# Gate and up of a feed-forward layer in two passes: plain products for the first half of the tokens, seven block products for the second, with weights and forms of x kept in DRAM

## The chip, the cores and the metric

The kernel runs on one core of one Trainium2 chip. The metric is the device time of one execution in microseconds, as the median of several runs. TensorE is PE in the profile, its weight loads PEld, VectorE is DVE, ScalarE is ACT, GpSimd is POOL and SyncE, which issues all transfers, is SP (SPq).

## The reference, cut to what matters

```
x = x + xattn(layernorm(x), ctx, ctx)        # 16 batches of 128 channels x 1024
h = layernorm(x)                             # 2048 tokens x 1024 features
Wg, Wu, Wd = NF4[codes] * scales             # 2752 x 1024, 2752 x 1024, 1024 x 2752; a scale for each 64 inputs
gate = einsum('bsh,ih->bsi', h, Wg)
up   = einsum('bsh,ih->bsi', h, Wu)
out  = x + einsum('bsi,hi->bsh', silu(gate) * up, Wd)
```

Everything is float32. The 2752 rows of the gate and up weights are 21 chunks of 128 and a half chunk of 64, which gate and up share.

## The kernel before

Three stages follow one another. The **mixer** is the attention: 16 batches, one per turn, on all engines; each turn ends with eight transposes of the normalized batch (x2), which ACT copies to `xh` in TensorE's rounded format and from which DVE makes the remainder `xl` (L823). The **gate and up stage** multiplies every chunk by the 2048 tokens, in four blocks (tb) of 512 tokens. A float32 product is three matmuls: weight high part by x high part, weight high by x low, weight low by x high (`products`, L1069 to L1071), eight times for the 1024 inputs. So 43 items (gate and up of 21 chunks, and the shared one) take 43 x 4 x 24 = 4128 matmuls. The **down stage** takes 40 groups of seven block products of six matmuls (`product`, L1116 to L1118) and 160 matmuls for the rest (L1125 to L1129). Its seven products stand for eight: sums of blocks of the stationary and moving operands are multiplied, and ACT (`snapshot`, L717) and DVE (L930) combine the results.

Beside the matmuls of the gate and up stage runs the making of weights. An item's codes and scales are loaded (L335, L340); ACT turns codes to levels in eight bends, each reading the last one's result (L578, L581); DVE multiplies by the scale (`weigh`, L767). For gate and up ACT makes the high part (L591) and DVE the low part (L772). For each finished block ACT takes silu of the gate (L648), DVE multiplies by up (L841), and SP stores the result (`inter`, L398). For the down stage one item of its weights is made per chunk. From two of them (a pair) seven *forms* are made, four of which are differences (`t_forms`); for each, ACT makes the high part (`form_hi`, L661), DVE the low part (`form_lo`, L846), and SP stores both together (L412). There is one buffer for a form, so `form_hi` waits until the store before it has landed (`form_stored`). Odd chunks make three forms, even chunks from 2 on make four: 70 in all.

The order on each engine is the order in which the program writes it down; nothing is reordered by a scheduler. Each engine goes through its own list and stops at the first wait that isn't met. SP does the same with transfers, all of which go through one queue.

## Time and profile before

| | |
|---|---|
| median of 3 runs | 1540.36 us (1540.14 to 1540.9) |
| the profiled execution | 1539.45 us, span 1537.7 us |
| PE busy | 1509.7 us, 98% of the span |
| ACT busy | 921.8 us, 60% |
| DVE busy | 724.2 us, 47% |
| DMA queue | 46.9% of 16 engines' span |

A duration of a matmul contains its way through the array, which the next matmul overlaps. What a matmul costs in a row of them is the distance from one start to the next. The same holds on ACT and DVE, where an instruction starts before the one ahead of it has ended if it doesn't need its result. "Landing" is the time from a transfer's issue on SP to its completion.

### The profile page before, as it was taken

The numbers are of one execution on the slowest core, as the hardware profiler recorded it, in microseconds if no ns is written. First come the engines' busy times: TensorE is split into PE (matmuls) and PEld (weight loads), VectorE is DVE, ScalarE is ACT, GpSimd is POOL, SyncE is SP. The second block draws the span as 40 slices with busy tenths as digits, with TensorE's granted clock in tenths as the row PEclk, the third lists the DMA queues.
The fourth block names the chain that finished last, engine by engine and source line by source line (L and its number), as shares of the span: only waits on it lengthen the run. The fifth ranks groups of instructions, "written<-read, shape, count | busy, mean of one in ns | idle before, by whom it ended". The sixth has DMA issues, their size and how long they took to land.

```text
span 1537.7 us, 18265 instructions
## 1 busy us (share of the span) xinstructions
PE 1509.7 (98%) x7056; PEld 1254.1 (82%) x7056; DVE 724.2 (47%) x1106; ACT 921.8 (60%) x1067; POOL 60.9 (4%) x99
## 2 busy tenths in 40 slices
PE   7999999999999999999999999999989999999998
PEld 6888788888888888888888888888768888888787
DVE  6998322322322222322322232222368888888764
...
DMA packets 115462, 232.93 MB, mean 151 GB/s; under 512 B 8240, under 2 KB 55344, under 8 KB 110896
## 3 DMA queue, kind: packets, MB, share of 16 engines
q1 hardware_dynamic: 115376, 231.77, 46.9%
...
q14 instruction: 30, 0.25, 0.1%
...
## 4 chain that ended last, share of the span: by engine, by line
PE 92%; ACT 4%; DMA 2%; issue 1%; DVE 1%; SPq 0%; DVEq 0%; POOL 0%; ACTq 0%
PE bank L1071 20%; PE bank L1069 20%; PE bank L1070 20%; PE bank L1116 8%; PE bank L1117 8%; PE bank L1118 8%; PE bank L1020 3%; PE bank L1047 1%; PE bank L1054 1%; DMA F<-inter_scratch 1%; PE bank L1037 1%; ACT early L602 1%; DMA inter_scratch<-F 1%; ACT F L615 1%; ACT F L636 1%
## 5 line engine op out<-in xcount | busy, mean ns | idle before, releaser
L1069 PE MATMUL bank<-R 128*128 128x512 f32 x1376 | 535.9, 389 | 0.0
L1070 PE MATMUL bank<-R 128*128 128x512 f32 x1376 | 535.7, 389 | 0.0
L1071 PE MATMUL bank<-R 128*128 128x512 f32 x1376 | 535.7, 389 | 0.0
L581 ACT ACTIVATE F<-F 128x1024 f32<-128x1024 f32 x441 | 467.6, 1060 | 13.3
L1070 PEld LDWEIGHTS bank<-R 128*128 128x128 f32 x1376 | 258.3, 188 | 53.7
L1071 PEld LDWEIGHTS bank<-R 128*128 128x128 f32 x1376 | 258.3, 188 | 53.6
L1069 PEld LDWEIGHTS bank<-R 128*128 128x128 f32 x1376 | 258.4, 188 | 53.3
L717 ACT COPY F<-bank 128x512 f32<-128x512 f32 x120 | 70.5, 587 | 271.0 <-PE bank L1118 267.1
L841 DVE TENSOR_TENSOR F<-F,bank 128x512 f32<-128x512 f32 x84 | 57.6, 686 | 331.1 <-issue 200.0
L648 ACT ACTIVATE F<-bank 128x512 f32<-128x512 f32 x84 | 49.8, 593 | 215.3 <-PE bank L1071 215.2
L767 DVE SCALAR_TENSOR_TENSOR F<-F 128x1024 f32<-128x1024 f32 x63 | 77.2, 1226 | 169.5 <-ACT F L581 169.5
L930 DVE TENSOR_TENSOR early<-early,bank 128x512 f32<-128x512 f32 x168 | 114.9, 684 | 36.0 <-PE bank L1129 23.9
L1118 PE MATMUL bank<-R 128*128 128x512 f32 x320 | 124.6, 389 | 0.0
L772 DVE TENSOR_TENSOR R<-F,R 128x1024 fp32r<-128x1024 f32 x41 | 50.2, 1225 | 154.9 <-ACT R L591 154.9
L846 DVE TENSOR_TENSOR F<-F 128x256 f32<-128x256 f32 (+2 forms) x230 | 121.0, 548 | 3.2 <-ACT F L661 1.1
L930 DVE TENSOR_TENSOR early<-early,F 128x512 f32<-128x512 f32 x120 | 82.6, 689 | 58.4 <-ACT F L717 57.9
L1118 PE MATMUL bank<-FR,R 128*128 128x512 f32 x240 | 94.6, 394 | 0.0
L1116 PE MATMUL bank<-R 128*128 128x512 f32 x232 | 90.6, 390 | 0.0
L1117 PE MATMUL bank<-R 128*128 128x512 f32 x232 | 90.5, 390 | 0.0
L1020 PE MATMUL bank<-ident,F 128*128 128x128 f32 x512 | 64.5, 279 | 9.9 <-DMA F<-in_ctx 5.8
L1116 PE MATMUL bank<-FR,R 128*128 128x512 f32 x168 | 66.5, 396 | 6.8 <-ACT F L717 6.8
L1118 PEld LDWEIGHTS bank<-R 128*128 128x128 f32 x320 | 60.2, 188 | 12.5
...
## 6 DMA issues: line engine op xcount, KB each, us to landing
wf_scratch<-F SPq DMA_DIRECT2D x70, 512.0 KB, 3.5
inter_scratch<-F SPq DMA_DIRECT2D x84, 256.0 KB, 2.3
F<-in_gu_codes SPq DMA_DIRECT2D x41, 512.0 KB, 5.0
F<-in_gu_scales SPq DMA_DIRECT2D x82, 256.0 KB, 4.2
F<-inter_scratch SPq DMA_DIRECT2D x40, 512.0 KB, 3.8
R<-wf_scratch SPq DMA_DIRECT2D x20, 1024.0 KB, 5.9
FR<-wf_scratch SPq DMA_DIRECT2D x15, 1024.0 KB, 5.9
F<-in_d_codes SPq DMA_DIRECT2D x22, 512.0 KB, 4.4
```

The lines of the kernel that those rows point to most:

```text
L581: nc.scalar.activation(y, y, ACT.Prelu, bias=bias, scale=scale, alpha=alpha).then_inc(bent, 1)
L717: nc.scalar.copy(snap[i], bankX[g % 2]).then_inc(ready, 1)
L767: nc.vector.scalar_tensor_tensor(dst, level[s], ZERO, scales[s], ALU.add, ALU.mult).then_inc(w_ready, 1)
L846: return nc.vector.tensor_tensor(out, x, y, ALU.subtract)
L930: return nc.vector.tensor_tensor(y, y, term, ALU.add)
L1020: i = pe.transpose(dst[:, t * P:(t + 1) * P], src[:, t * P:(t + 1) * P], ident[:, :])
L1069: pe.matmul(dst, hi, xh[:, tb, t, :], start=(t == 0), stop=False)
L1070: pe.matmul(dst, hi, xl[:, tb, t, :], start=False, stop=False)
L1071: i = pe.matmul(dst, lo, xh[:, tb, t, :], start=False, stop=(t == HT - 1))
L1116: pe.matmul(dst, h, moving[:, 0, k, :], start=start and k == 0, stop=False, skip_group_check=not start)
L1117: pe.matmul(dst, h, moving[:, 1, k, :], start=False, stop=False, skip_group_check=not start)
L1118: last = pe.matmul(dst, l, moving[:, 0, k, :], start=False, stop=k == 1, skip_group_check=not start)
```

## The change

- Gate and up run in two passes. The **first pass** is the plain one for tokens 0 to 1023 (blocks tb 0 and 1 of each chunk), in a position p for each chunk: 43 x 2 x 24 = 2064 matmuls. The order of the last positions is the table `BLOCKS`. `BX` is 8, half the batches.
- The **second pass** takes tokens 1024 to 2047. A position p is one chunk, gate and up together, as a product of 2 x 2 blocks (gate and up by the two halves of the inputs by the two blocks of tokens) in seven products of 12 matmuls (`pair_product`). The shared half chunk (p = 20, `FPOS`) takes four products; the last position is p = 21, `FULL`. That is 21 x 84 + 48 = 1812 matmuls.
- In the first pass only gate and up weights are made, two items per position, and each is also stored to `w_dram`. DVE and not ACT makes their high parts (`split`). Beside it the seven forms of x for the second half of the tokens are made, in 28 steps through the same one buffer `form`, 24 of which are stored to `xf_dram` and loaded again for the second pass.
- In the second pass a position loads its two weight items from `w_dram` (`load_staged`, 1 MB, one buffer `staged`), DVE makes four sums (`weight_sums`), ACT and DVE make high and low parts of the seven blocks (`wform_hi`, `wform_lo`), each into the slot that the same product of the position before has left. ACT copies three results (`snap1`, `snapq`, `snap2`), DVE adds others (`c11_sum`, `c22_sum`, `c21_sum`), ACT takes silu (`silu_c`, `silu_x`) and DVE multiplies (`pair_out`). The item of down weights per position, its eight bends and all 70 forms and their stores are now all here.
- In the mixer DVE makes `xl` for the first 8 batches only. The down stage has other buffers and banks; its loads are issued in another order.

The core of the diff; `snapq` and `snap2` are like `snap1`, `c22_sum` and `c21_sum` like `c11_sum`:

```diff
+    w_dram = nc.dram_tensor("w_scratch", (GU, P, N), F32).ap()
+    xf_dram = nc.dram_tensor("xf_scratch", (NP, P, 2, HT // 2, WIDE), F32).ap()
...
+        staged = f(4, 2)
+        tform = halves(6) + halves(7)
+        form = [v.bitcast(F32R) for v in halves(12)]
+        silu = halves(13)
+        inter = halves(14)
+        wsums = halves(15) + halves(16)
...
+        FPOS = FULL - 1
+        POS = FULL + 1
+        BLOCKS = [(p, tb) for p in range(FPOS) for tb in range(2)] + [(FPOS, 0), (FULL, 0), (FPOS, 1), (FULL, 1)]
+        NB1 = len(BLOCKS)
...
+        A11, A12, A21, A22 = [staged[:, i * WIDE:(i + 1) * WIDE] for i in range(4)]
+        WS1, WS2, WS3, WS4 = wsums
+        WFORMS = [A11, WS3, WS2, A12, WS1, A22, WS4]
+        pairX = [banks[0][:, 0, :], banks[1][:, 1, :]]
+        pairQ = [banks[0][:, 1, :], banks[2][:, 0, :]]
+        pairW = [banks[1][:, 0, :], banks[2][:, 1, :]]
...
+            def load_staged(p):
+                c = chunk_of(p)
+                if p:
+                    sp.wait_ge(wfl_ready, nth(p - 1, NP - 1))
+                if c == FULL:
+                    sp.dma_start(staged[:, 0:N], w_dram[GU - 1]).then_inc(staged_in, 16)
+                else:
+                    sp.dma_start(staged.rearrange("p (i n) -> p i n", i=2), w_dram[2 * c:2 * c + 2].rearrange("i p n -> p i n")).then_inc(staged_in, 16)
...
+            for p in range(POS):
+                if p:
+                    store_pair_out(p - 1, 1)
+                next_item(WN + 2 + p)
+                if p == KW:
+                    store_rest(0)
+                    sp.wait_ge(form_stored, 16 * 2 * NP)
+                    load_w(0, 0)
+                if p + 1 < POS:
+                    load_staged(p + 1)
+                for tb in range(4):
+                    store_form(p, tb)
...
+            def wform_hi(p, i):
+                if p == POS or i not in used(p):
+                    return
+                if p == 0:
+                    act.wait_ge(*((gate_done, 2 * FPOS + 3) if i < 4 else (up_done, ups_until(NB1 - 1))))
+                else:
+                    act.wait_ge(pair_done, nth(p - 1, i))
+                act.wait_ge(ws_ready, p + 1)
+                if p == FPOS:
+                    src = {0: A11, 1: WS3, 3: A12, 6: WS4}[i]
+                else:
+                    src = WFORMS[i]
+                nc.scalar.copy(wslice[i][:, 0], src).then_inc(wfh_ready, 1)
...
+            def snap1(p):
+                act.wait_ge(pair_done, nth(p, 0))
+                nc.scalar.copy(c11, pairX[p % 2]).then_inc(a1_ready, 1)
...
+                if last:
+                    bend_wd(FPOS, 2, 4)
+                else:
+                    bend_wd(p, 0, 1)
+                snap1(p)
+                form_hi(p, 0)
+                if last:
+                    bend_wd(FPOS, 4, 6)
+                else:
+                    bend_wd(p, 1, 2)
+                snapq(p)
+                form_hi(p, 1)
+                if last:
+                    bend_wd(FPOS, 6, 8)
+                else:
+                    bend_wd(p, 2, 3)
+                snap2(p)
+                if last:
+                    hi_a(0)
+                    hi_s(0)
+                bend_wd(p, 3, 4)
+                form_hi(p, 2)
+                wform_hi(p + 1, 0)
+                bend_wd(p, 4, 5)
+                silu_c(p)
+                wform_hi(p + 1, 1)
+                bend_wd(p, 5, 6)
+                wform_hi(p + 1, 2)
+                form_hi(p, 3)
+                bend_wd(p, 6, 7)
+                wform_hi(p + 1, 3)
+                bend_wd(p, 7, 8)
+            silu_x(FULL)
...
+            def split(n):
+                p, g = w_home(n)
+                par = p % 2
+                dve.wait_ge(w_ready, n + 1)
+                if p == 1:
+                    dve.wait_ge(fwl_ready, SLICES)
+                    dve.wait_ge(fw_stored, 16 * SLICES)
+                else:
+                    dve.wait_ge(up_done, 2 * p - 2)
+                nc.vector.tensor_copy(wgu[:, par, 0, g], w[n % 2]).then_inc(wh_ready, 1)
+                dve.wait_ge(wh_ready, n + 1)
+                nc.vector.tensor_tensor(wgu[:, par, 1, g], w[n % 2], wgu[:, par, 0, g].bitcast(F32), ALU.subtract).then_inc(wl_ready, 1)
...
+            def weight_sums(p):
+                dve.wait_ge(staged_in, 16 * (p + 1))
+                if p == FPOS:
+                    nc.vector.scalar_tensor_tensor(WS3, A11, -2.0, A11, ALU.mult, ALU.add)
+                    nc.vector.tensor_tensor(WS4, A11, A12, ALU.add).then_inc(ws_ready, 1)
+                    return
+                u = 2 * fulls(p)
+                nc.vector.tensor_tensor(WS1, A21, A22, ALU.add).then_inc(ws_step, 1)
+                sub(WS3, A11, A21)
+                dve.wait_ge(ws_step, u + 1)
+                sub(WS2, WS1, A11).then_inc(ws_step, 1)
+                dve.wait_ge(ws_step, u + 2)
+                sub(WS4, A12, WS2).then_inc(ws_ready, 1)
...
+            def c11_sum(p):
+                dve.wait_ge(pair_done, nth(p, 3))
+                dve.wait_ge(a1_ready, fulls(p) + 1)
+                nc.vector.tensor_tensor(c11, c11, pairW[p % 2], ALU.add).then_inc(c11_ready, 1)
...
+            for p in range(POS):
+                half, last = p == FPOS, p == FULL
+                if p:
+                    pair_out(p - 1, 1)
+                for i in range(4, NP):
+                    wform_lo(p, i)
+                if p and not last:
+                    weigh_wd(p)
+                    if p % 2:
+                        t_forms(p)
+                form_lo(p, 0)
+                form_lo(p, 1)
+                if last:
+                    s_forms(0)
+                    weigh_wd(p)
+                    lo_a(0)
+                    c11_sum(p)
+                    lo_s(0)
+                    c22_sum(p)
+                    c21_sum(p)
+                    pair_out(p, 0)
+                    break
+                weight_sums(p + 1)
+                if half:
+                    for i in range(3):
+                        wform_lo(p + 1, i)
+                    pair_out(p, 0)
+                    form_lo(p, 2)
+                    wform_lo(p + 1, 3)
+                    form_lo(p, 3)
+                    continue
+                form_lo(p, 2)
+                c11_sum(p)
+                wform_lo(p + 1, 0)
+                c22_sum(p)
+                wform_lo(p + 1, 1)
+                wform_lo(p + 1, 2)
+                form_lo(p, 3)
+                c21_sum(p)
+                pair_out(p, 0)
+                wform_lo(p + 1, 3)
+            pair_out(FULL, 1)
...
+            def pair_product(p, i, dst, start, stop):
+                wait(pe, wfl_ready, nth(p, i))
+                if p == 0:
+                    if i == DIRECT:
+                        pe.wait_ge(xpl_ready, XSTEPS)
+                    else:
+                        pe.wait_ge(xform_in[i], 16)
+                for j in range(HT // 2):
+                    hi, lo = [wslice[i][:, q, j * P:(j + 1) * P] for q in range(2)]
+                    a, b = start and j == 0, stop and j == HT // 2 - 1
+                    pe.matmul(dst, hi, xform[i][:, 0, j, :], start=a, stop=False, skip_group_check=not start)
+                    pe.matmul(dst, hi, xform[i][:, 1, j, :], start=False, stop=False, skip_group_check=not start)
+                    last = pe.matmul(dst, lo, xform[i][:, 0, j, :], start=False, stop=j == HT // 2 - 1, skip_group_check=not start)
+                last.then_inc(pair_done, 1)
...
+                pair_product(p, 0, X, True, True)
+                if p >= 2:
+                    pe.wait_ge(c21_ready, before)
+                pair_product(p, 1, Q, True, True)
+                pe.wait_ge(a1_ready, fulls(p) + 1)
+                pair_product(p, 2, X, False, True)
+                if p < 2:
+                    pe.wait_ge(blocks_done, 2 * FPOS + 3)
+                else:
+                    pe.wait_ge(c11_ready, before)
+                pair_product(p, 3, W, True, True)
+                pe.wait_ge(a2_ready, fulls(p) + 1)
+                pair_product(p, 4, X, False, True)
+                pe.wait_ge(aq_ready, fulls(p) + 1)
+                pair_product(p, 5, Q, False, True)
+                pe.wait_ge(c22_ready, fulls(p) + 1)
+                pair_product(p, 6, X, False, True)
...
-                if e:
+                if e and e.n < BX:
```

What stands in a row on three engines, before and after. On ACT, for one even chunk before: L578 and L581 are bends, L648 silu, L661 the high part of a form, L591 the high part of a gate or up weight.

```order
L578 ACTIVATE F<-F 128x1024 [waits w_ready,codes_in0]
L581 ACTIVATE F<-F 128x1024 [waits bent] x7
L648 ACTIVATE F<-bank 128x512 [waits blocks_done,gate_done]
L661 CAST F<-F 128x512 [waits form_stored,t_ready]
L578 ACTIVATE F<-F 128x1024 [waits w_ready,codes_in1]
L581 ACTIVATE F<-F 128x1024 [waits bent] x7
L648 ACTIVATE F<-bank 128x512 [waits blocks_done,gate_done]
L661 CAST F<-F 128x512 [waits form_stored,t_ready]
L578 ACTIVATE F<-F 128x1024 [waits w_ready,codes_in0]
L581 ACTIVATE F<-F 128x1024 [waits bent] x3
L591 ACTIVATE R<-F 128x1024 [waits up_done,w_ready]
L581 ACTIVATE F<-F 128x1024 [waits bent] x4
```

On ACT, in an even position of the second pass of the changed kernel (L805 and L808 bends, L857 the high part of a form, L872 the high part of a weight block, L876, L881 and L885 `snap1`, `snapq`, `snap2`):

```order
L805 ACTIVATE F<-F 128x1024 [waits w_ready,codes_in0]
L876 COPY F<-bank 128x512 [waits pair_done]
L857 CAST F<-F 128x512 [waits form_stored,t_ready]
L808 ACTIVATE F<-F 128x1024 [waits bent]
L881 COPY F<-bank 128x512 [waits pairs_out,pair_done]
L857 CAST F<-F 128x512 [waits form_stored,t_ready]
L808 ACTIVATE F<-F 128x1024 [waits bent]
L885 COPY F<-bank 128x512 [waits pair_done]
L808 ACTIVATE F<-F 128x1024 [waits bent]
L857 CAST F<-F 128x512 [waits form_stored,t_ready]
L872 CAST R<-F 128x512 [waits ws_ready,pair_done]
L808 ACTIVATE F<-F 128x1024 [waits bent]
```

The four forms of a position now stand between the snapshots that TensorE waits for, the first two of them ahead of `snap2`.

On DVE before, the end of one chunk and the start of the next (L767 weighs, L772 and L846 low parts, L841 silu by up):

```order
L772 TENSOR_TENSOR R<-F,R 128x1024 [waits wh_ready,w_ready]
L841 TENSOR_TENSOR F<-F,bank 128x512 [waits inter_stored1,up_done,silu_ready]
L846 TENSOR_TENSOR F<-F 128x512 [waits fh_ready]
L767 SCALAR_TENSOR_TENSOR F<-F 128x1024 [waits scales_in0,bent]
L772 TENSOR_TENSOR R<-F,R 128x1024 [waits wh_ready,w_ready]
L841 TENSOR_TENSOR F<-F,bank 128x512 [waits inter_stored0,up_done,silu_ready]
L846 TENSOR_TENSOR F<-F 128x512 [waits fh_ready]
L841 TENSOR_TENSOR F<-F,bank 128x512 [waits inter_stored1,up_done,silu_ready]
L846 TENSOR_TENSOR F<-F 128x512 [waits fh_ready]
```

On DVE in an even position of the second pass (L1050 weighs, L1144 subtractions for low parts of forms and weight blocks and for sums, L1205 the first weight sum, L1231 and L1236 `c11_sum` and `c22_sum`):

```order
L1260 TENSOR_TENSOR F<-F 128x512 [waits c22_ready,silux_ready,inter_stored1]
L1144 TENSOR_TENSOR R<-F,R 128x512 [waits wfh_ready] x3
L1050 SCALAR_TENSOR_TENSOR F<-F 128x1024 [waits scales_in1,bent]
L1144 TENSOR_TENSOR F<-F 128x512 [waits fh_ready] x2
L1205 TENSOR_TENSOR F<-F 128x512 [waits staged_in]
L1144 TENSOR_TENSOR F<-F 128x512
L1144 TENSOR_TENSOR F<-F 128x512 [waits ws_step] x2
L1144 TENSOR_TENSOR F<-F 128x512 [waits fh_ready]
L1231 TENSOR_TENSOR F<-F,bank 128x512 [waits a1_ready,pair_done]
L1144 TENSOR_TENSOR R<-F,R 128x512 [waits wfh_ready]
L1236 TENSOR_TENSOR F<-F,bank 128x512 [waits aq_ready,pair_done]
```

Both low parts of the first two forms now stand ahead of the weight sums, and these ahead of `c11_sum` and `c22_sum`.

On SP before, two blocks of one chunk (L398 stores inter, L412 a form, L335 and L340 load codes and scales):

```order
L398 DMA inter_scratch<-F 128x4x128 [waits blocks_done]
L412 DMA wf_scratch<-F 256x1x512 [waits fl_ready]
L335 DMA F<-in_d_codes 128x1024 [waits bent]
L340 DMA F<-in_d_scales 64x1024 [waits w_ready]
L340 DMA F<-in_d_scales 64x1024
L398 DMA inter_scratch<-F 128x4x128 [waits blocks_done]
L412 DMA wf_scratch<-F 256x1x512 [waits fl_ready]
```

On SP in an even position of the second pass (L494 stores inter, L421 and L426 load codes and scales, L535 is `load_staged`, L544 stores forms):

```order
L494 DMA inter_scratch<-F 128x4x128 [waits pairs_out] x2
L421 DMA F<-in_d_codes 128x1024 [waits bent]
L426 DMA F<-in_d_scales 64x1024 [waits w_ready]
L426 DMA F<-in_d_scales 64x1024
L535 DMA F<-w_scratch 128x2x1024 [waits wfl_ready]
L544 DMA wf_scratch<-F 256x1x512 [waits fl_ready] x4
L494 DMA inter_scratch<-F 128x4x128 [waits pairs_out] x2
```

The form stores now stand behind the scales and the 1 MB load of the next position's weights, four in a row.

## Rows read from the trace of the kernel before

**Rows 1.** Page: busy time, share, count; then the chain by engine.

```profile
PE 1509.7 (98%) x7056; PEld 1254.1 (82%) x7056; DVE 724.2 (47%) x1106; ACT 921.8 (60%) x1067; POOL 60.9 (4%) x99
...
PE 92%; ACT 4%; DMA 2%; issue 1%; DVE 1%; SPq 0%; DVEq 0%; POOL 0%; ACTq 0%
```

**Rows 2.** Windows: us, busy time and count per engine, clock, DMA share, GB/s.

```profile
163.80:1101.40 937.60, 937.30 (x4141) 776.19 (x4139) 260.82 (x314) 659.82 (x712) 0.74 (x2) 1.00 0.47 146
1101.40:1537.70 436.30, 421.46 (x1839) 346.92 (x1837) 327.47 (x542) 143.13 (x210) 0.00 (x0) 0.99 0.44 156
```

**Rows 3.** Timeline of PE: start, duration; stage start and stage end.

```profile
163.78 0.48 PE L1069 MATMUL bank<-R 128*128 128x512 f32 x1
...
1100.96 0.39 PE L1116 MATMUL bank<-FR,R 128*128 128x512 f32 x1
```

**Rows 4.** Timeline of PE: distance of matmuls at the lower clock.

```profile
1108.49 0.63 PE L1117 MATMUL bank<-FR 128*128 128x512 f32 x1
1108.91 0.63 PE L1118 MATMUL bank<-FR,R 128*128 128x512 f32 x1
```

**Rows 5.** Groups by line: the remainder of x in the mixer.

```profile
L823 DVE TENSOR_TENSOR R<-bank,R 128x1024 fp32r<-128x1024 f32 x16 | 19.5, 1219 | 3.5 <-ACT R L629 3.5
```

**Rows 6.** Timeline of ACT, 606 to 624 us.

```profile
606.12 0.60 ACT L648 ACTIVATE F<-bank 128x512 f32<-128x512 f32 x1 [1.16 <-PE bank L1071]
606.61 0.61 ACT L661 CAST F<-F 128x512 fp32r<-128x512 f32 x1
...
608.22 7.62 ACT L581 ACTIVATE F<-F 128x1024 f32<-128x1024 f32 x7
...
622.25 1.04 ACT L591 ACTIVATE R<-F 128x1024 fp32r<-128x1024 f32 x1
...
623.19 1.04 ACT L581 ACTIVATE F<-F 128x1024 f32<-128x1024 f32 x1
```

**Rows 7.** Timeline of DVE, 512- and 1024-wide operations in a row.

```profile
1112.60 0.68 DVE L930 TENSOR_TENSOR early<-early,bank 128x512 f32<-128x512 f32 x1
1113.20 1.22 DVE L846 TENSOR_TENSOR R<-F,R 128x1024 fp32r<-128x1024 f32 x1
1114.33 0.69 DVE L930 TENSOR_TENSOR early<-early,F 128x512 f32<-128x512 f32 x1
```

**Rows 8.** Timeline of SP: issue of a form store and the loads behind.

```profile
602.05 0.56 SPq L412 DMA_DIRECT2D wf_scratch<-F  x1
602.66 0.62 SPq L335 DMA_DIRECT2D F<-in_gu_codes  x1
606.24 1.16 SPq L340 DMA_DIRECT2D F<-in_gu_scales  x2
```

**Rows 9.** DMA issues at 602.05 and 617.7 us: landing; last, L419 by source.

```profile
wf_scratch<-F SPq DMA_DIRECT2D x1, 512.0 KB, 3.5
...
F<-in_d_scales SPq DMA_DIRECT2D x1, 256.0 KB, 4.2
...
DMA to landing us min/median/max: 4.7/5.9/18.6
```

**Rows 10.** Timeline of SP at 1064 us, then landings of its first and last issue.

```profile
1064.70 2.57 SPq L419 DMA_DIRECT2D FR<-wf_scratch  x4
...
1069.89 0.52 SPq L412 DMA_DIRECT2D wf_scratch<-F  x1
...
FR<-wf_scratch SPq DMA_DIRECT2D x1, 1024.0 KB, 5.9
...
wf_scratch<-F SPq DMA_DIRECT2D x1, 512.0 KB, 10.6
```

**Rows 11.** Windows at the entry of the down stage, columns as in Rows 2.

```profile
1104.00:1108.00 4.00, 0.99 (x4) 0.77 (x4) 0.69 (x1) 0.58 (x1) 0.00 (x0) 0.97 0.74 182
1108.00:1112.00 4.00, 4.00 (x12) 3.11 (x11) 2.91 (x7) 2.37 (x3) 0.00 (x0) 0.61 1.03 418
```

664 lines of the change are left out of this document (442 added, 222 removed).

## The prediction

> **What bounds the kernel now.** I read the busy shares first, then the chain of waits, both on the page [rows 1]: PE is busy 98% of the span and makes 92% of the chain that ended last. The reader is to see that nothing but fewer or cheaper matmuls can shorten it. The windows by stage say the same [rows 2]: from 163.8 to 1101.4 us PE is busy 937.3 of 937.6 us at clock 1.00, while ACT is busy 659.8 and DVE 260.8. The timeline of PE gives the price of a matmul: the stage's first starts at 163.78, the down stage's first at 1100.96 [rows 3]; less about 1.2 us for a mixer turn in between that is 936 us for 4128 matmuls, 0.2268 us each. ACT is the second engine (70% of the stage), so I looked up its prices by the distance of starts: a 512-wide copy or silu takes 0.5 us, a 1024-wide one 0.95 us if the next doesn't need its result [rows 6]. On DVE it is 0.6 us for 512 and 1.13 us for 1024 wide, and the result is there 0.7 or 1.2 us after the start [rows 7].
>
> **Matmuls.** Plain products of the second half cost 2064 x 0.2268 = 468 us. They become 1812 x 0.2268 = 411 us: 57 us less. The first pass keeps the other 2064, 468 us. That is the whole gain, and it stands only if PE doesn't wait.
>
> **First pass.** A position is 96 matmuls, 21.8 us. ACT has two items in it (16 bends; each needs the last one's result, and seven in a row take 7.62 us, so 1.09 us apart [rows 6], 17.4 us), two silus and two parts of x forms: 19.5 us. It fits by 2.3 us. DVE has about 10 us. The form store lands 3.5 us after its issue [rows 9], and x forms follow each other by some 10 us, so nobody waits. I cost the first pass at nothing beyond its matmuls. Were that cover gone, each 0.1 us per position would be 2 us.
>
> **Second pass, the period.** A full position is 84 matmuls, 19.05 us. ACT has eight bends at 0.95 and, in an even position, 16 operations at 0.5: 15.7 us. DVE has some 14 us. By busy time it fits. But each engine goes through its list in order, and two chains run through DMA. I follow one position with time 0 at the start of `silu_x` of the position before.
>
> Common start. ACT: silu 0, three weight blocks 0.5 to 2.0, bend 2.0, `snap1` 3.0. DVE: `pair_out` 0.65, three low parts from 1.25, `weigh` 3.05 to 4.3. SP issues the scales when `weigh` is done: 4.35 and 4.95, then `load_staged` at 5.55, then a form store at 6.1 (issue takes 0.56 to 0.62 us) [rows 8]. A scale load lands 4.2 us after its issue [rows 9], so 9.1. A 1 MB load lands 4.7 us after its issue at the least, 10.25 here [rows 9]. The queue works in order: four loads of 1 MB were issued from 1064.70; the first landed after 5.9 us, at 1070.6; the 0.5 MB form store issued at 1069.89 landed after 10.6 us, at 1080.5 [rows 10]. In between 3.75 MB landed (three loads, an inter store of 0.25 MB, this store), 2.6 us per MB. So `staged` lands between 10.25 and 9.1 + 2.6 = 11.7; I take 11.0, the middle. The form store behind it lands 1.3 later, 12.3 (11.5 to 13.0), instead of 9.6 alone.
>
> Odd position (three forms). The second form's high part waits for the first's store, 12.35. The weight sums start at 11.0 and, two of the four needing the one before, end at 13.7. From there ACT has a block (13.75), bend, `silu_c`, block, bend, block, the third form (17.9, when the second's store, issued 14.35, has landed), bend, block, bend: next `silu_x` at 20.8.
>
> Even position (four forms, in nine of them). The first form at 3.5 ends its low part at 4.9. The second waits until 12.35, and `snap2`, which stands behind it on ACT, is at 13.8 instead of 8.4; TensorE's fifth product waits for that, some 5 us. The third form needs high part 0.6, low part 0.7, store 3.5 and 0.1 between: 17.25. The fourth: 22.15. Bend, block, bend: next `silu_x` at 25.05. PE, with two products more behind `snap2` and the sixth-product sum `c22_sum` at 19.5, is done at about 23 and isn't the last. So a pair of positions takes 45.9 us, where plain products take 43.5 and the matmuls alone 38.1.
>
> **Entry and end of the second pass.** Position 0: the x forms of products 5 and 6 (2 MB each) are issued only when the first pass is done, and codes, scales and `load_staged(1)` stand behind them: 4 + 0.25 + 1 + 1 MB at 2.6 and 2 us of start, so 18.5 us after the pass ends; weight sums, `c11_sum`, a low part and `c22_sum` take 4.7 more. The seventh product starts at 23.3 instead of 16.3, and position 0 takes 27.7 us with ACT's rest. Positions 20 and 21: the first form store of 20 stands behind 2.5 MB, its four forms come at 2, 12.9, 19.3 and 24.4, the rest of the bends follow ahead of `snap1` and `snap2` of 21, and the last product ends near 44. Sum: 27.7 + 10 x 20.8 + 9 x 25.05 + 44 = 505 us against 468: **+37 us**.
>
> **Mixer.** Eight `xl` of 1.22 us [rows 5] go from DVE. PE's own transposes and products leave little room, so between 0 and -8; I take -3. Four small stores on SP hide.
>
> **Down stage.** It takes 436.3 us [rows 2] for 1840 matmuls, 417.3 us: 19 us of waits, lower clock and end. After the change weight slot 6 is loaded behind six 1 MB loads of x, so the seventh product waits some 7 us and the next group 3 more: between -8 and +5; I take -4.
>
> **Sum.** Against the profiled execution: 1539.45 + 37 - 3 - 4 = 1569.5. It was 0.9 below the median, 1540.36; so **1570 us**.
>
> **The rivals.**
> - *Transfers don't hold each other up.* For it: DMA is busy under half the time. Then `staged` lands at 10.25 and a store 3.5 us after issue: odd 20.0, even (9.65, 14.4, 19.2, then 2.9) 22.1; a pair is 42.1 and, with 3 us less at the ends, 1570 - 9.5 x 3.8 - 3 = **1531**. Against it: the 10.6 us of a store behind four loads [rows 10]. Chance 0.17. The Trainium skill speaks for this rival: DMA: Bandwidth & Descriptors, section Queues, rings and completion order, says that descriptors are taken in ring order but that completion is not first in, first out, so that a later transfer may be complete while an earlier one isn't. If that held for a form store behind `load_staged`, the time would be this rival's, by the order of rows 10 it is the forecast's.
> - *PE stays the bound*, the other side. If a form's wait moves nothing that PE needs, the second pass is 411 us and 5 at its entry: 1540.4 - 57 + 5 - 7 = **1481**. It needs fewer than 4.4 us per round of form and store; the row says 4.9. Chance 0.08.
> - *The lower clock.* After the idle stretch of 1104 to 1108 us the granted clock was 0.61 over the next 4 us [rows 11] and matmuls started 0.42 us apart [rows 4]. That is the lower of its two levels (1.2 against 2.4 GHz) for most of them. In even positions PE idles some 5 us before the fifth product. One slow product costs 2.4 us, which ACT's later end still covers; if all three behind the wait ran at it, they would end at 29.2 and nine positions cost 5 us more: **1612**. Chance 0.08.
>
> **How the numbers follow.** Forecast (1550 to 1590) 0.62, rivals 0.17, 0.08, 0.08, and 0.05 for what I haven't seen. The range reaches to the first rival and part of the third: 1520 to 1600. About 0.2%, 3 us, can be told from no change. Faster: 0.17 + 0.08 + 0.02 = 0.27; same 0.03; slower 0.70.
>
> **What would show it.** First pass: 468 us with no waits on PE, ACT above 85%. Second pass: `silu_x` starts alternate by about 21 and 25 us; ACT's largest wait is of `form_hi` for the DMA to `wf_scratch`; DVE waits for the DMA to `staged`; PE's waits stand before the fifth and seventh products, and its busy share in the pass is near 85%. A form store that lands 3.5 us after issue behind `load_staged`, or `snap2` on time in even positions, would make the forecast wrong.

## The result, and the profile after

| | before | after |
|---|---|---|
| median | 1540.63 us (1540.14 to 1542.16) | 1643.49 us (1640.49 to 1647.58) |
| ratio | | 1.0668, 95% interval 1.0638 to 1.0697 |
| the profiled execution | 1539.45 us | 1641.01 us, span 1639.3 |
| PE busy | 1509.7 us | 1492.3 us |

The change makes the kernel 103 us slower. 1570 us and a range of 1520 to 1600 were forecast: the direction came true, the size is 73 us off. First the page of after: its busy shares (against [rows 1]), DMA queue, chain, two of its costliest groups (busy, mean ns of one, then the idle time ahead and its releaser) and an issue group.

```profile
PE 1492.3 (91%) x6804; PEld 1230.7 (75%) x6804; DVE 958.4 (58%) x1479; ACT 997.8 (61%) x1268; POOL 60.9 (4%) x99
...
q1 hardware_dynamic: 135616, 302.03, 55.4%
...
PE 65%; DMA 14%; ACT 7%; DVE 7%; issue 3%; SPq 2%; ACTq 0%; DVEq 0%
...
L1539 PE MATMUL bank<-R 128*128 128x512 f32 x604 | 253.5, 420 | 107.7 <-ACT F L885 63.3
...
L857 ACT CAST F<-F 128x512 fp32r<-128x512 f32 x70 | 43.4, 620 | 164.1 <-DMA wf_scratch<-F 164.1
...
F<-w_scratch SPq DMA_DIRECT2D x21, 1024.0 KB, 8.2
```

PE's share of the chain has gone from 92% to 65%, and DMA's from 2% to 14%. PE is still busy for 91% of the span, but no longer everywhere. The windows of the three stages (against [rows 2]; length, busy us of PE, PEld, DVE, ACT, POOL, granted clock, DMA share, GB/s) tell where.

```profile
163.60:632.50 468.90, 468.90 (x2075) 388.44 (x2074) 193.25 (x224) 398.15 (x417) 0.74 (x2) 1.00 0.67 213
632.50:1193.60 561.10, 453.43 (x1815) 364.97 (x1813) 310.29 (x473) 337.37 (x496) 0.00 (x0) 0.89 0.55 180
1193.60:1637.60 444.00, 419.36 (x1840) 346.13 (x1838) 326.20 (x541) 142.73 (x209) 0.00 (x0) 0.98 0.45 164
```

The first pass is full of PE, to the microsecond. The second takes 561 us, of which PE is busy in 453 (81%), ACT in 337 and DVE in 310: no engine is near full there, and the pass is bound by a loop through several engines. The waits by engine, line and what was waited for (us, times, longest):

```profile
ACT F L857 <- DMA wf_scratch<-F: 164.1, 32, 11.8
...
DVE F L1205 <- DMA F<-w_scratch: 72.8, 10, 18.9
...
PE bank L1539 <- ACT F L885: 63.3, 9, 8.3
...
PE bank L1539 <- DVE F L1236: 32.0, 10, 9.9
...
ACT R L945 <- DMA F<-inter_scratch: 23.2, 1, 23.2
```

These are the waits that the prediction named: `form_hi` (L857) for the store of the form before it, the weight sums (L1205) for `staged`, and PE behind `snap2` (L885) and a block sum.

Position by position, by the starts of `silu_x` (L901): position 0 takes 31.6 us, odd positions 23.4 (mean of nine, 22.4 to 25.3), even ones 28.0 (mean of nine, 26.5 to 29.0), position 19 19.2, positions 20 and 21 together 47.3. Now two positions in detail. Timeline of SP in after (start, time of the issue, line, what, how many); `silu_x` starts at 819.0 ahead of an odd position and at 842.37 ahead of an even one.

```profile
820.85 0.51 SPq L421 DMA_DIRECT2D F<-in_d_codes  x1
823.38 1.16 SPq L426 DMA_DIRECT2D F<-in_d_scales  x2
824.59 0.60 SPq L535 DMA_DIRECT2D F<-w_scratch  x1
826.64 14.73 SPq L544 DMA_DIRECT2D wf_scratch<-F  x3
...
847.93 0.59 SPq L535 DMA_DIRECT2D F<-w_scratch  x1
848.56 0.56 SPq L544 DMA_DIRECT2D wf_scratch<-F  x1
```

`load_staged` (L535) is issued 5.6 us after `silu_x` in both; the prediction's figure was 5.55. What it released, on DVE and on ACT:

```profile
832.73 0.69 DVE L1205 TENSOR_TENSOR F<-F 128x512 f32<-128x512 f32 x1 [6.12 <-DMA F<-w_scratch]
...
858.59 0.62 ACT L857 CAST F<-F 128x512 fp32r<-128x512 f32 x1 [10.18 <-DMA wf_scratch<-F]
```

The landings of the loads issued at 824.59 and 847.93 and of the store issued at 848.56 (KB, us from issue to landing):

```profile
F<-w_scratch SPq DMA_DIRECT2D x1, 1024.0 KB, 8.1
...
F<-w_scratch SPq DMA_DIRECT2D x1, 1024.0 KB, 9.3
...
wf_scratch<-F SPq DMA_DIRECT2D x1, 512.0 KB, 10.0
```

That is the whole error in small: 8.1 and 9.3 us where 5.45 was taken, and 10.0 for the form store behind it where the prediction had 6.2. Position 8, the even one shown, is one of the later cases. Over the nine odd and the nine even positions the load lands after 8.0 and 8.1 us on average (6.5 to 9.3), and the first form store of an even position after 8.8 (7.2 to 10.0). Counted from `silu_x`, the load has landed at 13.5 and 13.8, and the second form of an even position begins at 15.1.

### The profile page after: what moved, and what is told of

Its sections match the earlier page's. It is cut to its first block, busy times and chain, and to the rows that moved or that the text cites. A ratio compares the mean times of both kernels' runs of the same rounds, so it can differ in the third digit from the quotient of the medians.

```text
span 1639.3 us, 18807 instructions
## 1 busy us (share of the span) xinstructions
PE 1492.3 (91%) x6804; PEld 1230.7 (75%) x6804; DVE 958.4 (58%) x1479; ACT 997.8 (61%) x1268; POOL 60.9 (4%) x99
## 4 chain that ended last, share of the span: by engine, by line
PE 65%; DMA 14%; ACT 7%; DVE 7%; issue 3%; SPq 2%; ACTq 0%; DVEq 0%
PE bank L1494 10%; PE bank L1495 10%; PE bank L1493 10%; PE bank L1582 8%; PE bank L1584 7%; PE bank L1583 7%; DMA wf_scratch<-F 7%; DMA F<-w_scratch 5%; PE bank L1441 3%; PE bank L1539 2%; ACT F L808 2%; DVE R L1144 2%; PE bank L1540 2%; PE bank L1541 2%; DVE F L1144 2%
## 5 line engine op out<-in xcount | busy, mean ns | idle before, releaser
L1539 PE MATMUL bank<-R 128*128 128x512 f32 x604 | 253.5, 420 | 107.7 <-ACT F L885 63.3
L1493 PE MATMUL bank<-R 128*128 128x512 f32 x688 | 268.2, 390 | 0.0
L1494 PE MATMUL bank<-R 128*128 128x512 f32 x688 | 268.0, 389 | 0.0
L1495 PE MATMUL bank<-R 128*128 128x512 f32 x688 | 268.0, 389 | 0.0
L1540 PE MATMUL bank<-R 128*128 128x512 f32 x604 | 249.6, 413 | 0.0
L1541 PE MATMUL bank<-R 128*128 128x512 f32 x604 | 248.3, 411 | 0.0
L1144 DVE TENSOR_TENSOR F<-F 128x256 f32<-128x256 f32 (+2 forms) x305 | 169.4, 582 | 130.3 <-ACT F L857 127.5
L1539 PEld LDWEIGHTS bank<-R 128*128 128x128 f32 x604 | 122.5, 203 | 143.2 <-ACT F L885 67.1
L1144 DVE TENSOR_TENSOR R<-F,R 128x512 fp32r<-128x512 f32 (+2 forms) x215 | 164.9, 785 | 16.7 <-ACT R L872 16.5
L1050 DVE SCALAR_TENSOR_TENSOR F<-F 128x1024 f32<-128x1024 f32 x63 | 77.1, 1223 | 139.5 <-ACT F L738 124.8
L808 ACT ACTIVATE F<-F 128x1024 f32<-128x1024 f32 x147 | 155.6, 1058 | 0.1
L1582 PE MATMUL bank<-FR,R 128*128 128x512 f32 x336 | 131.9, 392 | 21.4 <-ACT F L957 21.4
L1493 PEld LDWEIGHTS bank<-R 128*128 128x128 f32 x688 | 129.2, 188 | 26.8
L1494 PEld LDWEIGHTS bank<-R 128*128 128x128 f32 x688 | 129.2, 188 | 26.7
L1495 PEld LDWEIGHTS bank<-R 128*128 128x128 f32 x688 | 129.2, 188 | 26.7
L857 ACT CAST F<-F 128x512 fp32r<-128x512 f32 x70 | 43.4, 620 | 164.1 <-DMA wf_scratch<-F 164.1
L1541 PEld LDWEIGHTS bank<-R 128*128 128x128 f32 x604 | 122.0, 202 | 27.2
L1540 PEld LDWEIGHTS bank<-R 128*128 128x128 f32 x604 | 122.7, 203 | 25.8
L1583 PE MATMUL bank<-FR,R 128*128 128x512 f32 x336 | 131.4, 391 | 0.0
```

What stands on the lines that cost most here:

```text
L808: nc.scalar.activation(y, y, ACT.Prelu, bias=bias, scale=scale, alpha=alpha).then_inc(bent, 1)
L1144: return nc.vector.tensor_tensor(out, x, y, ALU.subtract)
L1493: pe.matmul(dst, hi, xh[:, tb, t, :], start=(t == 0), stop=False)
L1494: pe.matmul(dst, hi, xl[:, tb, t, :], start=False, stop=False)
L1495: i = pe.matmul(dst, lo, xh[:, tb, t, :], start=False, stop=(t == HT - 1))
L1539: pe.matmul(dst, hi, xform[i][:, 0, j, :], start=a, stop=False, skip_group_check=not start)
```

## The experiments

Theory A, from the traces: each position has three limits and takes the longest. They are the time of the weights (from `load_staged` on), the time of the forms (each waits for the store before it), and what is left with neither of the two (PE, ACT and the sums between them). The prediction's chains were right and one duration, the staged load's landing, was too short. The rivals: one of the two DMA chains is the only cause; the lower clock after PE's waits carries a good part; SP's queue order itself, and not what the transfers share, delays them.

### The two limits apart and together

**e_staged_first**: `load_staged` is issued ahead of the item's codes and scales.

```diff
+                if p + 1 < POS:
+                    load_staged(p + 1)
                 next_item(WN + 2 + p)
...
-                if p + 1 < POS:
-                    load_staged(p + 1)
```

> One line of SP's list is moved: the load of the next position's weights (L535, 1 MB) is issued ahead of codes and scales instead of behind them. In the changed kernel it lands 8.1 us after its issue in an odd position and the form store behind it 10 us after its own in an even one; silu_x starts lie 23.4 (odd) and 28.0 us (even) apart. Theory A, one queue in order: weights land by about 9.5 us of a position instead of 13.7, the first form store by about 10.5 instead of 16.2; odd positions take about 20.5, even ones about 23.5, the kernel about 1643 - 9.5 x 7.4 = 1573 us (1560 to 1590). Theory B, the lower clock after PE's idle stretches makes the loss: PE still idles before the fifth product, so under 20 us are won. Theory C, the sum of the transfers (4.3 MB per position) is the limit: the order changes nothing, 1640.

Measured 1602.75 us (1601.17 to 1604.97), ratio 1.0402 (1.0388 to 1.0417): 41 us less than the changed kernel, not the expected 70. Odd positions take 20.8 us, even ones 26.8; the staged load lands in 4.9 us. None of the three ranges holds it. The odd positions came as A had them. The even ones did not: codes and scales now stand right ahead of the first form's store, which still lands 8.2 us after its issue, and the second form begins at 13.8 and not near 10.5.

**e_two_forms**: a second form buffer, used in turn, so that a form waits for the store before the last.

```diff
+        form2 = [R2[:, 7 * N + h * WIDE:7 * N + (h + 1) * WIDE] for h in range(2)]
...
-                wait(act, form_stored, 16 * k)
-                nc.scalar.copy(form[0], src).then_inc(fh_ready, 1)
+                wait(act, form_stored[k % 2], 16 * (k // 2))
+                nc.scalar.copy(dform[k % 2][0], src).then_inc(fh_ready, 1)
```

> The forms of down weights get a second buffer (the unused last eighth of R2), each with a semaphore of its own, so that a form waits for the store before the last one. SP's order is that of the changed kernel. Theory A (form waits on ACT hold the snapshots in even positions, the late load of weights holds all): the 16 us wait in even positions goes, even positions become like odd ones, 23.4 us, so 9 x 4.6 = 41 us less: about 1602 us; odd positions stay, since DVE still waits for the weights. Theory B (the clock): PE's long gaps before the fifth product vanish, the clock stays near 1.00, and the odd positions get shorter as well: under 1590. Theory C (sum of transfers): 1640.

Measured 1601.83 us (1596.59 to 1605.84), ratio 1.0393 (1.0372 to 1.0415), as expected. Odd positions 23.8, even ones 24.4.

**e_both**: both edits.

> Both edits together: weights loaded ahead of codes and scales, and two form buffers. Theory A: every position comes down to about 20 us (19.05 of matmuls plus what is left between weight sums, the c22 sum and the seventh product), so 19 x 5.7 = 108 us less than 1643: about 1535 us (1520 to 1550), level with the kernel before. Theory B and C: the gains don't add, 1560 or more.

Measured 1520.31 us (1516.78 to 1523.2), ratio 0.9865 (0.9849 to 0.9882): 1.3% less than before the change, and as theory A had it. Odd positions 18.3, even ones 21.5. One edit alone gives 41 or 42 us, the two 123. The waits of the first, the second and of both, for the same two things:

```profile
ACT F L857 <- DMA wf_scratch<-F: 137.7, 32, 10.6
...
DVE F L1205 <- DMA F<-w_scratch: 20.3, 10, 14.9
```

```profile
DVE F L1211 <- DMA F<-w_scratch: 151.5, 20, 19.2
```

```profile
DVE F L1211 <- DMA F<-w_scratch: 33.8, 20, 14.9
...
ACT R L862 <- DMA wf_scratch<-R: 22.1, 6, 4.9
```

Each edit alone leaves the other wait in place, and DVE's wait for `staged` even grows from 72.8 to 151.5 us, since it now comes in the even positions too (20 times, not 10). The positions follow a maximum of three limits: weights 23.8 (odd) and 24.4 (even), forms 20.8 and 26.8, the rest 18.3 and 21.5. By that the changed kernel would have 23.8 and 26.8; it has 23.4 and 28.0. The two limits aren't independent: in the changed kernel the form's store stands behind the load, and the second form begins at 15.1 and not at 13.8, which are the 1.2 us that the maximum lacks in even positions. So both limits are real, and neither rival of a single cause stands.

**e_form0_first**: the first form's store ahead of the staged load. Only even positions have a form at this place (tb 0), so the edit leaves the order of the odd ones as it was.

```diff
+                store_form(p, 0)
                 if p + 1 < POS:
                     load_staged(p + 1)
-                for tb in range(4):
+                for tb in range(1, 4):
```

> The changed kernel with one thing moved: in the second pass SP issues the store of the first form of a position ahead of the load of the next staged weights, not behind it. In the changed kernel the second form of an even position begins 16.2 us after silu_x (842.4 to 858.6), because the first form's store stands behind the staged load, which stands behind the item's loads. Theory A (the store waits its turn in SP's queue, so the order of the two sets who is late): the second form begins some 10 to 11 us after silu_x, but the staged load moves 2 us later in each position; the odd positions lose up to 2 us (23.4 to 25), the even ones gain 2 to 4 us of their 28.0; time 1625 us (1600 to 1650), that is, a small gain or none, far from the 123 us that both edits together brought. Theory B (only the form round bounds the second pass): gain in the even positions of the whole 5 us, the odd ones unchanged, 1590 to 1600 us.

Measured 1602.83 us (1597.92 to 1605.64), ratio 1.0408 (1.0391 to 1.0426): 41 us less. That lies inside A's range, but is nearer to B's number, and the pattern is B's: even positions went from 28.0 to 23.6, nearly the whole 5 us, odd ones from 23.4 to 23.0. What B supposed, that the forms alone bound the pass, is refuted by e_both all the same; with this order the even positions come down to the limit of the weights. The even positions' first store and the load that is now behind it:

```profile
833.34 0.60 SPq L544 DMA_DIRECT2D wf_scratch<-F  x1
833.98 0.61 SPq L535 DMA_DIRECT2D F<-w_scratch  x1
```

```profile
wf_scratch<-F SPq DMA_DIRECT2D x1, 512.0 KB, 5.3
...
F<-w_scratch SPq DMA_DIRECT2D x1, 1024.0 KB, 6.9
```

The store lands after 5.3 us (also the mean; 8.8 in the changed kernel), and the load doesn't lose what A feared: it is issued 0.6 us later and lands after 7.5 us on average in place of 8.1, which is 13.8 us after `silu_x` in both kernels. The swap gives the store 4 us and costs the load nothing.

### What makes the staged load late

Three kernels keep codes, scales, queue order and waits, and change what the scale loads of the second pass bring. Each replaces the inner `sp.dma_start` of `load_scales` there. **e_plain_scales** reads different rows of x in the shape of before:

```diff
-                    sp.dma_start(scales[slot][h * BLOCK:(h + 1) * BLOCK, :],
-                                 src[h:h + 1, :].to_broadcast([BLOCK, ITEM])).then_inc(scales_in[slot], 16)
+                        sp.dma_start(scales[n % 2][h * BLOCK:(h + 1) * BLOCK, :],
+                                     x[0, h * BLOCK:(h + 1) * BLOCK, :]).then_inc(scales_in[n % 2], 16)
```

> The changed kernel, with the two scale loads of each item of the second pass reading 2 x 64 different rows of x in place of one row of scales repeated over the partitions: same bytes, same queue place, same waits. The numbers that they bring are not the scales, so the weights computed in this pass are others; the work is the same. It asks what makes the staged load land 8.1 us after its issue in the odd positions of the changed kernel, where 5.45 us were assumed. Theory A (the repeated rows are slow to read, and the staged load queues behind them: the records of 826 to 828 show only some 200 GB/s with the DMA share at 0.7 to 0.9): the staged load lands about 5.5 to 6 us after its issue, the odd positions fall from 23.4 to about 21 us, the even ones by a little less, and the time comes to 1590 us (1575 to 1610). Theory B (it queues behind the bytes ahead of it and shares the engines with the form's store, whatever rows the scales come from): staged load within 0.5 us of 8.1 us, time within 0.4% of 1643 us.

Measured 1633.51 us (1625.71 to 1639.27), ratio 1.0598 (1.0559 to 1.0636). The staged load lands after 7.5 us in odd and 8.1 in even positions (8.0 and 8.1 in the changed kernel); odd positions take 22.7, even ones 27.6. Repeating a row is not the cause; the 10 us that it may cost lie between the two theories, near B.

**e_small_scales** cuts each to an eighth:

```diff
+                        sp.dma_start(scales[n % 2][h * BLOCK:(h + 1) * BLOCK, 0:128],
+                                     d_scales[wd_tile(n - WN)][h:h + 1, 0:128].to_broadcast([BLOCK, 128])).then_inc(scales_in[n % 2], 16)
```

> The changed kernel, with each scale load of the second pass cut to its first 128 of 1024 columns (32 KB in place of 256 KB, still a row repeated over 64 partitions). The other columns keep older scales, so the down weights are others; the work is the same. Queue order, issue times and waits stay. In the changed kernel the staged load issued at 824.59 lands 8.1 us later, and with rows that are not repeated it took 8.3 us, so repeating isn't it. Theory A (the staged load lands behind the bytes that are still to be moved ahead of it: at 2.6 us per MB, 0.44 MB less are 1.1 us, and less still in flight when it is issued): it lands 5.5 to 7 us after its issue, a position is 1 to 2.5 us shorter, the time is 1610 us (1590 to 1630). Theory B (what holds it is something else than the loads ahead, say the form store and x forms beside it): it lands within 0.5 us of 8.1 us and the time stays within 0.6% of 1643 us.

Measured 1594.21 us (1591.05 to 1595.61), ratio 1.0342 (1.0326 to 1.0358), 49 us less. The landing of the staged load issued at 804.05:

```profile
F<-w_scratch SPq DMA_DIRECT2D x1, 1024.0 KB, 5.6
```

On average it is 5.7 us in odd and 6.1 in even positions; odd positions take 20.9, even ones 26.0. This is theory A: the load is late by what is ahead of it in flight. But 0.44 MB of scales were worth 2.0 to 2.3 us, about 5 us per MB, where the prediction counted 2.6. The windows of after show the slow stretch (columns as above):

```profile
826.00:827.00 1.00, 1.00 (x7) 0.81 (x6) 0.61 (x2) 0.54 (x1) 0.00 (x0) 1.00 0.92 209
827.00:828.00 1.00, 1.00 (x6) 0.84 (x5) 0.00 (x0) 0.81 (x2) 0.00 (x0) 1.00 0.72 193
...
829.00:830.00 1.00, 1.00 (x6) 0.81 (x5) 0.00 (x0) 0.00 (x0) 0.00 (x0) 1.00 0.93 324
830.00:831.00 1.00, 1.00 (x6) 0.84 (x5) 0.00 (x0) 0.00 (x0) 0.00 (x0) 1.00 0.98 379
```

The second load of scales lands at 828.4. In the two windows before, the engines are busy for 0.92 and 0.72 of the time and bring 209 and 193 GB/s; later, at 0.93 and 0.98, they bring 324 and 379.

They also get out of step. The packets of the form store behind the load are the only ones of 2 KB in this stretch, and I take an engine that starts on one to be done with its part of the load. In the changed kernel the first of them starts 2.7 us before the load lands (mean of the 16 loads between 690 and 1090 us, 0.9 to 3.7), with the small scales 1.0 us (0.7 to 1.4). The load's landing fell by 2.2 us over the same loads, and this lag between the first and the last engine by 1.7. Read so, most of the delay is that some engines are done with their share much later than others.

**e_plain_wide** brings the same bytes over 128 partitions:

```diff
+                        sp.dma_start(scales[n % 2][:, h * WIDE:(h + 1) * WIDE],
+                                     x[0, :, h * WIDE:(h + 1) * WIDE]).then_inc(scales_in[n % 2], 16)
```

> The changed kernel, with the two scale loads of each item of the second pass (64 partitions x 4 KB each, one row repeated) replaced by two loads of 128 partitions x 2 KB of different rows of x: same bytes, same two issues at the same place. The numbers brought are not the scales, so the weights are others; the work is the same. With different rows in the old shape (64 partitions x 4 KB) the staged load landed 8.3 us after its issue, and with an eighth of the bytes 5.6 us. Theory A (64 partitions load the DMA engines unevenly, and the staged load's last part stands behind the fullest): over 128 partitions it lands 6 to 7 us after its issue and the time is 1600 to 1622 us. Theory B (the half MB costs this much in any shape): it lands within 0.5 us of 8.1 us and the time is 1625 to 1650 us.

Measured 1635.57 us (1633.48 to 1638.84), ratio 1.0613 (1.0595 to 1.063): theory B. The load issued at 823.49 releases DVE at 831.92, 8.4 us later; the means are 8.2 and 8.7. Neither the repeated row nor the 64 partitions make the half MB slow. Why it is slow, and why it sets the engines apart, stays open.

**e_pool_staged**: GpSimd issues the staged loads, at the same event.

```diff
-                if p + 1 < POS:
-                    load_staged(p + 1)
...
+            for p in range(POS - 1):
+                c = chunk_of(p + 1)
+                pool.wait_ge(wfl_ready, nth(p, NP - 1))
+                if p + 2 < KT:
+                    pool.wait_ge(w_ready, WN + 1 + p)
...
+                    nc.gpsimd.dma_start(staged.rearrange("p (i n) -> p i n", i=2), ...).then_inc(staged_in2, 16)
```

> The changed kernel, with the staged loads of the second pass issued by GpSimd, whose queue carries nothing else, at the same event as before (the scales' event, and the last low part of the position's weight slices). SP keeps codes, scales, form stores and inter stores. It asks whether a transfer is held by its queue's order or by the 16 DMA engines that all queues share. Theory A (order in one queue: a load that has a queue of its own lands in the 4.9 us that it takes when it stands first in SP's queue, and the form store, with nothing of 1 MB ahead of it, lands some 4 to 5 us after its issue): odd positions near 20 us, even ones near 24, time 1565 us (1545 to 1585). Theory B (the engines are shared, so bytes issued at the same time wait for each other in whatever queue): staged lands 7.5 us or more after its issue, positions within 1 us of 23.4 and 28.0, time 1625 to 1650 us.

Measured 1622.27 us (1616.68 to 1625.31), ratio 1.0515 (1.0489 to 1.0541). Odd positions 22.8, even ones 27.2. The issues from 700 to 1100 us:

```profile
F<-w_scratch POOLq DMA_DIRECT2D x16, 1024.0 KB, 8.7
```

8.7 us to landing against 8.2 in SP's queue over the same stretch: theory B's landing and positions. The time is 21 us less, just under B's range and far from A's. Of this the issue explains a part: GpSimd doesn't stand behind SP's issues of the scales and starts the load 4.9 us after `silu_x` and not 5.6; what the rest is, no run shows. A queue of its own doesn't help a transfer whose bytes go through the same 16 engines. The Trainium skill says so too (DMA: Bandwidth & Descriptors, section Issuing engines are not separate DMA queues): transfers started by different engines end up on the same 16 DMA engines. The trace agrees with these 8.7 us.

**e_one_scale**: the two scale loads of an item as one, in all stages.

```diff
-                for h in range(2):
-                    sp.dma_start(scales[slot][h * BLOCK:(h + 1) * BLOCK, :],
-                                 src[h:h + 1, :].to_broadcast([BLOCK, ITEM])).then_inc(scales_in[slot], 16)
+                sp.dma_start(scales[slot],
+                             src.unsqueeze(1).to_broadcast([2, BLOCK, ITEM])).then_inc(scales_in[slot], 16)
```

> The changed kernel, with the two scale loads of an item (256 KB each, one row repeated over 64 partitions) made one load of 512 KB over all 128 partitions; same bytes, one issue less on SP, in all stages. Cutting the scales to an eighth of their bytes took the staged load from 8.1 to 5.6 us after its issue and 49 us off the time, more than 0.44 MB by 2.6 us per MB (1.1 us) explain. Theory A (each load of 64 partitions uses the DMA engines unevenly, so the two cost more than their bytes): one load over 128 partitions lands sooner, the staged load behind it lands 6 to 7 us after its issue, and the time is 1610 us (1595 to 1625). Theory B (the 0.5 MB themselves, however they are cut): the staged load is issued 0.6 us earlier and still lands near 8 us after it, the time is 1625 to 1650 us.

Measured 1968.96 us (1963.31 to 1971.54), ratio 1.2774: 325 us more, where both theories said less or the same. More than half of it arises in the first pass, which has two items per position: the first matmul of the second pass starts at 811.6 us and not 632.5. The second pass takes 143 us more, the down stage the same. Windows after the issue of such a load at 922.26, with the staged load at 922.87 behind it:

```profile
928.00:929.00 1.00, 1.00 (x6) 0.84 (x5) 0.00 (x0) 0.00 (x0) 0.00 (x0) 1.00 0.99 315
929.00:930.00 1.00, 1.00 (x6) 0.81 (x6) 0.00 (x0) 0.00 (x0) 0.00 (x0) 1.00 0.74 283
930.00:931.00 1.00, 1.00 (x6) 0.84 (x5) 0.00 (x0) 0.00 (x0) 0.00 (x0) 1.00 0.12 49
931.00:932.00 1.00, 1.00 (x7) 0.81 (x6) 0.00 (x0) 0.00 (x0) 0.00 (x0) 1.00 0.13 53
...
937.00:938.00 1.00, 0.00 (x0) 0.00 (x0) 0.00 (x0) 0.00 (x0) 0.00 (x0) 1.00 0.13 51
```

From 930 to 938 us the DMA share is 0.12 to 0.14, two engines of 16, at some 50 GB/s. The staged load lands only at the end of this stretch, 15.5 us after its issue: it has a part on the two engines that are still at the scales. The Trainium skill has the rule (DMA: Bandwidth & Descriptors, section Why a DMA increments its semaphore by 16 and not by 1): a transfer runs on the largest number of engines, up to 16, that divides the outermost size above 1 of both of its access patterns. Here that size is 2 on the source's side, and the trace shows two engines. So this run doesn't tell what it was made for, but it shows bare the mechanism: a transfer lands when the last of its engines has done all that is ahead of it. **e_best_one_scale**, the same edit in the fastest version, took 1829.78 us (1827.41 to 1837.37) in place of 1504. There the staged load goes ahead of the scales and still lands after 4.8 to 5.6 us; it is the first two form stores of a position, behind the scales, that take 10 to 17 us. Both theories of this expectation were wrong:

> The fastest version so far (1503.9 us: staged load ahead of the item's loads, second form buffer, y loads behind the stage loads, seventh x form behind the staged load) with the one scale load over 128 partitions. There the positions alternate by 17.9 and 21.4 us, TensorE is busy 378 of 400 us between 700 and 1100 us, and nothing waits long for the scales. Theory A (a scale load no longer bounds anything there): within 0.3% of 1504 us. Theory B (uneven loads still slow the form stores and slice loads around them): 1490 to 1499 us.

### The clock

**e_fill2**: matmuls in PE's wait ahead of the fifth product of even positions.

```diff
+                if p % 2 == 0 and p >= 2:
+                    for _ in range(20):
+                        pe.matmul(banks[3][:, 0, :], xform[1][:, 0, 1, 0:P], xform[1][:, 0, 0, :], start=True, stop=True)
                 pe.wait_ge(a2_ready, fulls(p) + 1)
```

> The changed kernel with 20 matmuls on the same tile, into a bank that nobody reads before it is started anew, put on TensorE ahead of the fifth block product of each even position from the third on (9 positions): there TensorE waits 5.9 us (801.7 to 807.6) for ScalarE's copy L885, after which the granted clock reads 0.50 for some 6 us. The 20 products take 4.5 us of that wait. Theory A (the clock after the wait costs little, since TensorE catches up before silu_x, which waited for it 0.3 to 1.4 us): time within 0.5% of 1643 us, and the granted clock over 700:1100 us up from 0.89 to 0.95 or more. Theory B (the lower clock carries a good part of the 73 us by which the forecast was missed): 14 columns of work at half clock are 2.8 us in each of 9 positions, so at least 25 us less: 1618 us or below.

Measured 1634.07 us (1629.2 to 1635.53), ratio 1.0599 (1.0581 to 1.0617). The profiled executions lie 6.5 us apart. Windows from 700 to 1100 us of after and of this kernel:

```profile
700.00:1100.00 400.00, 328.05 (x1307) 264.08 (x1308) 232.02 (x354) 250.35 (x369) 0.00 (x0) 0.89 0.53 171
```

```profile
700.00:1100.00 400.00, 355.70 (x1479) 286.75 (x1480) 235.85 (x360) 253.85 (x376) 0.00 (x0) 0.96 0.55 175
```

The granted clock rose from 0.89 to 0.96, and the time fell by 9 us, 0.6%: a little above A's 0.5%, far from B's 25 us. The lower clock is real (after the wait of 801.7 to 807.6 us it reads 0.50 over 808 to 812 us, the lower of the two levels) and explains an eighth of the miss at most. Even that is generous: the even positions, where the matmuls stand, went from 28.0 to 27.8 us, 2 us in all, and position 0, ahead of the first of them, was 2 us shorter as well. What the 0.04 below full clock that is left costs was not tried.

### The entry of the down stage, and the fastest version

**e_all** is e_both with six of eight y loads (`early<-x_scratch`) behind the second stage load.

> As the one before, and four of the six 1 MB loads of x at the entry of the down stage are issued behind the second stage load instead of ahead of the last stores of inter. In the changed kernel ACT waits 23.2 us there for the stage load (issued at 1215 us) and PE 21.2 us. Theory A: the last stores and weight slot 6 no longer stand behind 6 MB at 2.6 us each; some 10 us of the 21 go: 1525 us (1512 to 1540), faster than the kernel before. If the wait is for something else (the last inter stores land late by themselves), it gives under 3 us.

Measured 1519.3 us (1515.01 to 1521.69), ratio 0.9857 (0.9839 to 0.9874): 1 us less than e_both, whose interval it shares. By the expectation this said that the wait at the entry is for something else. PE's waits there tell another story:

```profile
1091.36 0.79 PE L1588 MATMUL bank<-FR,R 128*128 128x512 f32 x1 [12.86 <-ACT F L962]
1109.11 0.80 PE L1588 MATMUL bank<-FR,R 128*128 128x512 f32 x1 [6.56 <-ACT F L962]
```

The first wait was 22.25 us in e_both. It fell by 9.4, and a second of 6.56 came up: the next stage load, issued at 1090.48, now has six y loads of 1 MB ahead of it and not two, landed 17.2 us later (9.7 in e_both), and ACT waited 8.65 us for it. Most of the wait was moved, not taken away, so this run didn't decide what its expectation asked. **e_best** goes further:

```diff
-                    for m in range(6):
-                        load_y(m)
...
             load_stage(1)
-            for m in range(6, NM):
+            for m in range(2):
                 load_y(m)
...
                     load_stage(g + 2)
+                if g + 2 < NM:
+                    load_y(g + 2)
```

and in position 0 `load_xform(6)` stands behind `load_staged(1)`.

> The version with the staged load ahead of the item's loads and with a second form buffer (1520.3 us), and three more edits of SP's order: in position 0 the seventh form of x is loaded behind the staged load, not ahead of it; the six early loads of y, which stand ahead of the last inter stores and of the second stage's load at the entry of the down projection, are put behind that load (two of them), the others each behind the stage load of its step. Theory A (the entry's wait of 20 to 23 us on ScalarE and TensorE comes from the y loads ahead of the stage loads): the entry gives back 10 to 15 us, position 0 some 3 us: 1505 us (1498 to 1512). Theory B (the entry waits for the store of the last inter tiles, whose landing no order of the loads shortens; moving only some of the y loads brought 1 us): 1516 to 1521 us.

Measured 1503.92 us (1501.58 to 1505.96), ratio 0.976 (0.9745 to 0.9774): theory A. PE at the entry, in e_both and in e_best:

```profile
1101.88 0.80 PE L1588 MATMUL bank<-FR,R 128*128 128x512 f32 x1 [22.25 <-ACT F L962]
```

```profile
1078.09 0.80 PE L1589 MATMUL bank<-FR,R 128*128 128x512 f32 x1 [8.66 <-ACT F L963]
1082.95 0.80 PE L1589 MATMUL bank<-FR,R 128*128 128x512 f32 x1 [1.94 <-DVE early L1324]
```

22.25 us of wait (19.4 in e_all) are 10.6. The other edit takes position 0's end from 662.8 to 655.8, 7 us. With them e_best is 37 us faster than the kernel before the change: in its second pass odd positions take 17.9 us and even ones 21.4.

## Why the prediction was right and wrong

- **Bound, price of a matmul.** Right. The price from [rows 1 to 3] was 0.2268 us; the first pass was to be 468 us without a wait of PE, and is 468.9. The shape of ACT's and DVE's lists in the first pass held as well.
- **The form of the second pass.** Right: alternating positions, the waits of L857 and L1205, PE late behind `snap2` (5.9 us from 801.7; "some 5 us"), the issue of `load_staged` 5.6 us after `silu_x`.
- **"`staged` lands between 10.25 and 11.7; I take 11.0."** This is the step that failed. It landed 13.5 us after `silu_x` in odd positions and 13.8 in even ones (means; 12.5 to 14.9). The low end was the fastest landing of a 1 MB load [rows 9], the high end the scales' landing plus 2.6 us per MB from [rows 10], where four loads of 1 MB follow one another. With codes and scales in flight ahead, the same megabyte took 8.0 and 8.1 us on average and not 5.45. In the position that begins at 819.0 the scales landed at 9.4, much as worked out (9.1); the load came 4.3 us behind them and not 2.6 at most. e_staged_first (4.9), e_small_scales (5.7 and 6.1) and the half MB of other rows (7.5 to 8.7) measure the term. Everything behind it carried on as worked out: 13.5 + 9.8 (the prediction's 20.8 - 11.0) = 23.3, measured 23.4.
- **"The form store behind it lands 1.3 later, 12.3."** The 1.3 was right, the landing that it is added to was the same term again. The store lands at 15.05 on average, 1.3 behind the load. The second form of an even position begins at 15.1 after `silu_x`, not 12.35; plus the 12.7 us that were worked out from there on, 27.8, measured 28.0. Nine odd positions at 2.6 and nine even ones at 2.95 more are 50 of the 73 us.
- **Position 0, the last positions.** 31.6 for 27.7 and 47.3 for 44, less 1.6 us in position 19, whose staged load has half the bytes and lands in 4.7 us: 6 us together. Sum of the pass: 561 for 505.
- **The down stage, -4 us.** Wrong in sign. From 1193.6 us on it takes 445.7 us and not 432. The prediction looked at weight slot 6 behind six loads of 1 MB, and not at the last inter stores and the second stage load that stand behind them too: that load was issued 21.5 us after `silu_x`, at 1215.07, and ACT waited 23.2 us for it. This is 13 us. One transfer of the three that the y loads hold up had been costed.
- **The mixer, -3 us.** The first matmul of gate and up starts at 163.62 and not 163.78 [rows 3]: the DVE work of [rows 5] had been hidden. 3 us. In the profiled execution 56 + 13 + 3 = 72 us, against 1641.01 - 1569.5 = 71.5; the median lies another 2 us above what was added for it.
- **The rivals.** Transfers that don't hold each other (1531) fell: the store behind `load_staged` took 7.4 and 10.0 us. In all nine even positions the load landed first and the store behind it, as in [rows 10]. PE as the bound (1481) fell, but e_best with 1504 shows that it lies near once both limits are gone. The lower clock is worth 9 us at most; its price in the prediction was also added up wrongly, since nine times 5 us on 1570 are 1615 and not 1612.
- **The range** ended at 1600 because both ends of the landing came from loads with loads of their own kind ahead. No row of a 1 MB load behind codes and scales was used, and the high end was no bound. The direction was forecast for the right reason; of the 103 us only some 30 were.
